# Indirect DMAs in the head attention of a hybrid layer: one wait for each head's scores in place of one for two heads

## The reference

```python
def _L0_attn_b_ref(x, ...):                       # 16 heads of 64
    q, k, v = (einsum('bsd,hpd->bhsp', x, w) + b for w, b in ...)
    scores = einsum('bhqp,bhkp->bhqk', q, k) / sqrt(64)
    attn = softmax(scores, axis=2)                # over the queries
    ctx = einsum('bhqk,bhkp->bqhp', attn, v)
    return ctx.reshape(b, s, 16 * 64) @ l_w.T + l_b

def _L0_ffn_ref(x, ...):                          # 8 experts, top 2, capacity 160 a sequence
    buf.at[e_flat, b_idx, pos_c].add(x_rep * keep)        # tokens to their slots
    y = relu(buf @ W1 + b1) @ W2 + b2
    y_tok = y[e_flat, b_idx, pos_c] * keep * p_flat       # answers back to tokens
    return y_tok.reshape(B, T, 2, C).sum(axis=2)

x = x + attn_a(layernorm(x)); x = x + ffn(layernorm(x))
x = x + attn_b(layernorm(x)); x = x + ffn(layernorm(x))
```

## Time and profile before

| | us |
|---|---|
| median of 3 runs | 1502.43 |
| lowest, highest | 1499.57, 1503.81 |
| span of the profiled execution | 1499.3 |
| PE busy in it | 1445.1 (96%) |
| DVE busy | 1063.7 (71%) |
| ACT busy | 919.5 (61%) |
| POOL busy | 280.3 (19%) |
| scatters in attention (L1752), 64 instructions | 62.7 |
| first gathers (L1711), 32 instructions | 32 x about 1.0 |

### The profile page before, as it was taken

How to read it: one execution, slowest core, us unless ns; L and a number is a source line. 1 busy time by engine, 2 the same in 40 slices (tenths; PEclk the granted TensorE clock), 3 DMA queues, 4 the chain that set the end, 5 groups by cost and what they waited for, 6 DMA issues and landing times.

```text
span 1499.3 us, 43267 instructions
## 1 busy us (share of the span) xinstructions
PE 1445.1 (96%) x18426; PEld 1004.5 (67%) x18426; DVE 1063.7 (71%) x2172; ACT 919.5 (61%) x1727; POOL 280.3 (19%) x325
## 2 busy tenths in 40 slices
PE   7999789999999999999999999999999999999996
PEld 6988774565677675656777756557777565467486
DVE  6884037887666679877666788776667887777754
ACT  5765566656666666566666666666666665666553
POOL 4165613013210012130000120400000213000055
PEclk9999999999999999999999999999999999999999
DMA  8501221001110011010000110110001101100002
GB/s 223 192 19 57 67 61 38 22 23 46 28 30 16 16 42 33 23 48 16 16 16 16 40 32 22 34 47 16 16 16 39 32 23 34 47 16 16 1 19 57
DMA packets 44461, 58.27 MB, mean 39 GB/s; under 512 B 8231, under 2 KB 32656, under 8 KB 44144
## 3 DMA queue, kind: packets, MB, share of 16 engines
q1 hardware_dynamic: 35120, 38.27, 9.4%
q0 software_dynamic: 9152, 17.26, 4.1%
HBM read 22.14 MB, written 19.32 MB: 28 GB/s over the span
## 4 chain that ended last, share of the span: by engine, by line
PE 86%; DVE 7%; ACT 3%; issue 2%; another core or an unknown queue 2%; DMA 0%; DVEq 0%; ACTq 0%
PE bank L1134 29%; PE bank L1147 26%; PE bank L1057 6%; PE bank L1062 4%; PE bank L1071 3%; PE bank L434 3%; PE bank L406 3%; DVE nmx L1169 3%; PE bank L1289 2%; PE bank L1285 2%; ACT prob L1178 2%; PE bank L1246 1%; ACT hT L528 1%; DVE stats L1330 1%
## 5 line engine op out<-in xcount | busy, mean ns | idle before, releaser
L1178 ACT ACTIVATE prob<-bank,nmx 128x1024 f32<-128x1024 f32 x512 | 570.3, 1114 | 427.3 <-DVE nmx L1169 426.4
L1169 DVE TENSOR_REDUCE nmx<-bank 128x1 f32<-128x1024 f32 x512 | 625.8, 1222 | 210.2 <-PE bank L1134 193.7
L1147 PE MATMUL bank<-prob,vsc 64*64 64x512 f32 x4096 | 644.9, 590 | 4.6 <-DVE ctxT L1196 2.7
L1134 PE MATMUL bank<-q,k 64*64 64x512 f32 x2048 | 530.4, 592 | 6.6 <-ACT prob L1178 5.5
L1134 PE MATMUL bank<-q,ks 64*64 64x512 f32 x2048 | 527.4, 591 | 0.0
L1147 PEld LDWEIGHTS bank<-prob,vsc 64*64 64x64 f32 x4096 | 232.3, 133 | 130.6 <-issue 64.3
L1057 PE MATMUL bank<-xT,wqkv_sb 64*64 64x256 f32 (+1 forms) x1560 | 210.3, 435 | 0.0
L1134 PEld LDWEIGHTS bank<-q,ks 64*64 64x64 f32 x2048 | 137.0, 133 | 81.0 <-issue 26.8
L1741 POOL DMA_INDIRECT yg<-yslots,row_ring x64 | 64.5, 1008 | 609.3 <-PE bank L1134 581.5
L1134 PEld LDWEIGHTS bank<-q,k 64*64 64x64 f32 x2048 | 133.9, 133 | 46.8 <-ACT prob L1178 16.6
L1057 PEld LDWEIGHTS bank<-xT,wqkv_sb 64*64 64x64 f32 x1560 | 90.3, 133 | 89.3 <-issue 39.7
(11 more groups left out here) (270 smaller groups left out, 1619.7 us busy)
## 6 DMA issues: line engine op xcount, KB each, us to landing
ks<-k SPq DMA_DIRECT2D x62, 256.0 KB
yslots<-slots_sb SPq DMA_DIRECT2D x7, 640.0 KB, 3.6
slots_sb<-xslots SPq DMA_DIRECT2D x5, 640.0 KB, 4.8
xslots<-xhat_r POOLq DMA_DIRECT2D x5, 512.0 KB, 7.3
yslots<-xhat_r POOLq DMA_DIRECT2D x5, 512.0 KB, 12.4
w_sb<-in_w SPq DMA_DIRECT2D x1, 2048.0 KB, 9.0
wqkv_sb<-in_wqkv SPq DMA_DIRECT2D x1, 2048.0 KB, 19.1
xslots<-xhat_r,row_s POOLq DMA_INDIRECT x112
```

The lines of the kernel that those rows point to most:

```text
L1134: ins = nc.tensor.matmul(bank[rows(c), SC[h][n], :], kk[r, cols(2 * j + c, HD)], qst[pi % 2][r, cols(n, HALF)], start=True, stop=True)
L1147: ins = nc.tensor.matmul(bank[rows(h), CX[n], :], vsc[s][rows(r), rows(h)], prob[g % 3][h][rows(r), cols(n, HALF)], start=(j == 0 and firs ...
L1169: nc.vector.tensor_reduce(nmx[:, 2 * s + h:2 * s + h + 1], bank[:, SC[h][0]:SC[h][0] + 2, :], mybir.AxisListType.XY, ALU.max, negate=True) ...
L1178: nc.scalar.activation(prob[g % 3][h][:].rearrange("p (n c) -> p n c", c=HALF), bank[:, SC[h][0]:SC[h][0] + 2, :], ACT.Exp, bias=nmx[:, 2 ...
```

## The change

`paced` takes the head for which it waits. With h = 1 it waits as before; with h = 0 it waits for one signal less, the first head's scores of the same step. In `first_gather(p, 1)` and `c_scatter` each DMA now has its own wait: even ones for head 0, odd ones for head 1. `first_gather(p, 2)` and `c_gather` stay as they are.

```diff
-        def paced(p, g):
-
-            hold(p, c_qk, 2 * min(g + 3, LAST + 1))
+        def paced(p, g, h=1):
+
+            hold(p, c_qk, 2 * min(g + 3, LAST + 1) - 1 + h)
...
                     if fb == 2:
                         paced(p, 31 + c)
-                    elif t % 2 == 0:
-                        paced(p, 1 + c // 2)
+                    else:
+                        paced(p, 1 + c // 2, c % 2)
...
             for k in range(2):
                 for t in range(T):
-                    if t % 2 == 0:
-                        paced(p, b * STEPS + 22 + (k * T + t) // 2)
+                    c = k * T + t
+                    paced(p, b * STEPS + 22 + c // 2, c % 2)
```

## The result

The changed kernel takes 1487.12 us (median of 4 runs, 1484.56 to 1491.49) against 1501.0 us for the kernel before (4 runs, 1499.25 to 1503.81): ratio 0.9908, 95% interval 0.9886 to 0.993, so 10.5 to 17.1 us less, 13.8 at the ratio itself. The forecast was 9.5 us less and 1492.9 us, with a range from 1488.5.

What follows compares the result with a forecast made beforehand. TensorE, busy 96% of the span, bounds the kernel, losing time to late signals beside paired DMAs. 13.2 - 3.7 = 9.5 us less takes the profiled 1499.3 to 1489.8; adding 3.1 to reach the median gives 1492.9 us, range 1488.5 to 1504.

Steps and rivals of the forecast that it cites:

- Part (1): 40 added waits on GpSimd, 32 at scatters and 8 at gathers: cost nothing; without cover, each under 0.30 us.
- Part (2): Removing 40 doublets (two DMAs behind one wait) at scatters and first gathers: 13.2 us less, 0.33 us each.
- the slower rival: Every DMA holds signals until 1.48 us, like the second of a pair: +8, 1510; chance 0.12.
- Part (3): In plain steps the first DMA holds signals until 1.36 us; head 1's maximum is 0.46 us late, free for PE.
- maximum 1: VectorE's maximum of head 1's scores, its signal due 0.90 us after the step's first DMA; 0.62 us lateness free.
- Part (4): Steps where VectorE is late already pass on 0.46 us whole: 8 x 0.46 = 3.7 us lost.
- 8 tight steps: Two in each of sequences 1 to 3, two at first gathers: norm or combining work meets evacuation or head-pair end.
- A and B: First and second DMA of a step, behind head 0's and head 1's scores; forecast to start 2.17 us apart.
- every DMA holds as the second of a doublet: Rival at the attention's DMAs: signals held until 1.48 us after each start, lateness grows; +8, 1510; chance 0.12.
- Half: Rival: a step's first DMA holds like a single, its second like a pair's second; 4.9 less, 1497.5; chance 0.12.
- The doublets aren't the cause, or their cost moves: Rival: scatter stretches' loss is norm and routing work, or moves to head 1's maximum; 1502.4; chance 0.24.
- (2) whole: Best case: the whole cost of the paired DMAs comes off, 13.2 us less, 1489.2.

Runs made afterwards that it cites:

- g1: Changed kernel without the 64 scatters of the head attention, counter steps in their place (answers wrong); 1487.96 us.
- h1_after: The changed kernel itself, on a chip where no signals are held; 1460.1 us against 1459.95 for the kernel before, ratio 1.0004.
- i1: Changed kernel with each step's first DMA waiting one signal earlier, then for memsets, to start about 0.15 us earlier; 1489.02 us.
- f4: Changed kernel with a 128x32 GpSimd memset after every wait for both heads' scores; 1491.06 us.
- f3: Changed kernel with a 128x720 GpSimd memset ahead of every DMA that waits for the second head; 1489.6 us.
- f2: Changed kernel with DMAs paired again, both behind the first head's scores, no wait for the second; 1501.82 us.
- batches e and h: Two series of experiments on chips where no output piece is held; kernel before 1459.94 and 1459.95 us.
- g3: Changed kernel with two GpSimd memsets ahead of each of the 80 DMAs; 1489.64 us.
- i2: Kernel before with a 128x720 GpSimd memset between the two DMAs of a pair, one wait for both heads; 1489.11 us.

## Why the prediction was right and wrong, point by point

**What bounds the kernel, and where the loss sits**: right. The stretches picked from the windows view gave up 12.7 us; the rest of the span is unchanged within 0.5 us.

**Part (1), 40 added waits cost nothing**: right. The attention part is within 0.8 us of g1's, which has no scatters at all (1177.9 against 1177.1).

**Part (2), 13.2 us of doublets**: right. The four scatter terms, 3.02, 3.53, 3.48 and 1.85, add up to 11.9; the trace without scatters puts them at 3.34, 3.42, 3.38 and 1.84, which is 12.0. The deductions for transposing pieces, combining and norm work were right within 0.35 us a sequence. The gathers, 1.31, gave 1.69: their reference of 39.07, steps of the second sequence, was 0.39 too long. The stretch is 38.69 us after the change, and 38.68 in h1_after, where nothing is held. The nine steps with single gathers take 39.07 us in h1_after too, so the 0.15 us that the prediction put down to their holds, and used again for norm work and as evidence against the slower rival, is no cost of held signals.

**Part (3), A's hold catches maximum 1**: this is the step that failed. The signal was due 0.90 us behind A and came at 0.85, as worked out. But the hold until 1.36 us was read from one row, an output piece, and carried over to the signal of scores. At that distance 59 of 60 output pieces are held in the changed kernel and none of 33 scores; i1 shows that scores mostly pass at 1.01 as well. The signals differ by kind, and the prediction took a row of one kind for another. So B's wait was not late either, and A and B stand 1.72 us apart and not 2.17.

**Part (4), 8 tight steps, 3.7 us**: hence mis-sized. Each was to pay the 0.46 us of maximum 1, and there is no such lateness. The scatter stretches keep 1.0 us over their floor and the first gathers kept nothing. And that 1.0 lies elsewhere, half of it in sequence 4, which the prediction left out. There the change does not keep two DMAs apart, at the start of a head pair (POOL, then DVE, then the chain):

```profile
1234.93 0.97 POOL L1752 DMA_INDIRECT xslots<-xhat_r,row_s  x1 [1.18 <-PE bank L1134]
1236.37 0.97 POOL L1752 DMA_INDIRECT xslots<-xhat_r,row_s  x1 [0.47 <-issue]
```

```profile
1237.79 0.69 DVE L1196 COPY ctxT<-bank 128x512 f32<-128x512 f32 x1 [0.93 <-PE bank L1147]
```

```profile
1235.72 1.27 PE bank L1071 x5
```

Two starts are 1.44 us apart. The copy of the context starts 1.42 us behind the second, and the half-projection's piece lasts 1.27 us where the same piece ahead took 0.23: its increment comes at 1236.99, 0.62 us behind the second start, and PE waits for it. This is the long hold once more, and with 0.46 us of delay in that step it is nearly all of the 0.48 us of sequence 4. In f4 the same two starts are 1.73 us apart, in f3 1.86, and sequence 4 is at the floor in both. The other half, 0.1 to 0.3 us in each of sequences 1 to 3, was not traced to a signal.

**The sum**: 13.2 - 3.7 = 9.5 was forecast. With the terms as measured it is 13.7 - 1.0 = 12.7. The rest of 13.8 is within the spread between executions; the interval begins at 10.5 and holds 12.7, and not 9.5.

**The rivals**: *every DMA holds as the second of a doublet* fell: 34 held scores before, none after. *Half* fell with it, as no signal of head 0 is held by 0.3 us. *The doublets aren't the cause, or their cost moves* fell for this change. In f2 it came true: the cost moved, mostly to the half-projection's signals, and grew (16.5 us over the floor in the four stretches, against 12.0 before). The Trainium skill, "SBUF — State Buffer", says of the two sides of SBUF that they cannot contend. The time on the chips of batches e and h (1.0004) agrees with what the prediction drew from it, that spreading DMAs gives nothing; on the others the time does not (0.991). The page speaks of ports and not of signals, so this is no measurement against what it says of ports.

**The range**: its lower end rested on (2) whole, 1489.2, and 0.7 us more. With one run more the median of before went from 1502.43 to 1501.0, and the gathers gave 0.4 us more than the term; that put the result under it. A best case should carry the spread of the runs downward as well as upward.

## What to carry to other kernels

Where a trace shows a matmul piece far longer than its twin just behind indirect DMAs of GpSimd, compare the piece's length with the start of the consumer: the work may be done and only its signal late. In this kernel pairs of indirect DMAs 1.28 us apart cost 0.34 us each (13.7 us for 40) and those some 1.7 us apart or more next to nothing, so part them, best by letting each wait for an event of its own; moving a close pair elsewhere in the step can change no more than who pays. Compare on more than one chip: on two of these the change is worth nothing. And read a delay from a row with the same kind of signal as the one it is used for.

## What was not expected of the hardware

- Chips differ. The kernel before takes 1460 us on the chips of two batches and 1499 to 1502 on those of three, with holds of signals only on the latter. Of the 40 us that the kernel before takes longer there, 15 lie in the attention (1190.6 us, against 1176.0 in h1_after); of the changed kernel's 27 it is 2 (1177.9). The changed kernel's attention begins at 200.9 us in h1_after and at 220.3 on the first chip. There the granted clock falls to the lower of its two levels (1.2 in place of 2.4 GHz) for 17 us in all between 128 and 193 us, and for 14 us in the kernel before, which a page of tenths does not show; in h1_after it stays at the upper level until 1454 us. By an estimate from these rows, at half speed that is at most 8 or 9 of the 19.4 us. In the attention both run at the upper level, so the clock is not what holds signals there. The rest was not studied.
- Beside indirect DMAs, signals of TensorE came up to 1.6 us late (f2, half-projection) while matmuls that did not need them ran on. Plain DMAs in pairs, 0.53 us each on POOL, cost nothing.
- Which mechanism holds a signal, and why a single start holds output pieces and hardly ever scores, stays open. The time since the start is not the only reason (i1), nor is the place in the step (g3).
- A DMA behind a memset starts little later than without one (1.03 us behind the signal in place of 0.87, for a memset of 0.70 us), and with memsets on GpSimd DVE is busy longer: 50.72 us in i2's third sequence against 49.02 in the changed kernel.
